# Two-layer graph network on one core: ScalarE copies the edge counts of sixteen destinations in one instruction instead of eight

## The reference, cut to what matters

```python
norm = dis[src] * dis[dst]
def _gcn(x, W, b, src, dst, norm):
    h = x @ W
    msg = h[src] * norm[:, None]
    out = jax.ops.segment_sum(msg, dst, num_segments=N)
    return out + b
h = jax.nn.relu(_gcn(x, W1, b1, src, dst, norm))
h = jax.nn.relu(_gcn(h, W2, b2, src, dst, norm))
return (x + h) * 0.5
```

## Time and profile before

| what | value |
|---|---|
| three runs | 1050.73, 1050.91, 1060.28 us; median 1050.91 |
| the profiled execution | 1058.88 us |
| its span, first to last instruction | 1057.0 us |
| mean granted TensorE clock | 0.956 of full speed |
| busy, TensorE matmuls / weight loads | 953.4 / 635.5 us |
| busy, VectorE / ScalarE / GpSimd | 698.6 / 591.3 / 442.9 us |
| copies out of the windows (L1611) | 784 instructions, 348.1 us |

### The profile page before, as it was taken

The page is one execution under the profiler, slowest core; times in us unless marked ns, Lnnn a source line. Parts: engine busy times, 40 slices in busy tenths (PEclk is TensorE's granted clock), DMA queues, the critical chain, the costliest instruction groups (busy, mean ns, idle before and its releaser), DMA issues.

```text
span 1057.0 us, 24147 instructions
## 1 busy us (share of the span) xinstructions
PE 953.4 (90%) x9848; PEld 635.5 (60%) x9848; DVE 698.6 (66%) x1238; ACT 591.3 (56%) x1322; POOL 442.9 (42%) x260
## 2 busy tenths in 40 slices
PE   5666677579979999999999999999999999999996
PEld 4566676466756666766666665555555555555554
DVE  5688788599969999999999990233333333333333
ACT  4999354289869989898988982112222222212212
POOL 3688304239864868959682000301222222212220
PEclk9898889659989999999999999999999999999997
DMA  9999999106663556666554501346766776777700
GB/s 326 385 389 378 361 323 319 34 27 197 223 226 118 173 162 223 223 223 198 165 173 154 186 2 36 111 153 232 240 232 231 238 239 232 239 239 239 240 27 18
DMA packets 196421, 214.97 MB, mean 203 GB/s; under 512 B 5359, under 2 KB 172421, under 8 KB 196174
## 3 DMA queue, kind: packets, MB, share of 16 engines
q1 hardware_dynamic: 190621, 201.05, 56.1%
q0 software_dynamic: 4944, 10.51, 3.1%
q10 hardware_dynamic: 737, 1.77, 0.4%
HBM read 137.71 MB, written 72.39 MB: 199 GB/s over the span
## 4 chain that ended last, share of the span: by engine, by line
PE 68%; POOL 6%; DVE 3%; ACT 3%; issue 1%; DMA 0%; POOLq 0%
PE dense_p L1655 44%; PE win_p L1647 10%; POOL ql L1314 4%; PE win_p L1745 4%; PE win_p L1736 2%; PE win_p L1753 2%; DVE st L1486 2%; POOL ql L1319 1%; ACT uv L1525 1%; PE lin_p L1712 1%; PE win_p L1721 1%; PE lin_p L1672 1%; DVE adj_all L1486 1%; ACT adj_all L1611 1%; PE code_p L1635 1%
## 5 line engine op out<-in xcount | busy, mean ns | idle before, releaser
L1611 ACT CAST adj_all<-win_p 128x392 f16<-128x392 f32 x784 | 348.1, 497 | 42.7 <-PE win_p L1647 17.5
L1655 PE MATMUL dense_p<-adj_all,g_all 128*128 128x448 f16 x1372 | 364.1, 352 | 0.2 <-ACT adj_all L1611 0.2
L1647 PEld LDWEIGHTS win_p<-adj_all,st 128*128 128x128 f16 x3136 | 215.6, 101 | 135.2 <-DVE adj_all L1486 17.8
L1655 PE MATMUL dense_p<-adj_all,total 128*128 128x448 f16 x1372 | 275.1, 353 | 0.0
L1647 PE MATMUL win_p<-adj_all,st 128*128 128x98 f16 x3136 | 256.7, 213 | 15.2 <-DVE adj_all L1486 9.9
L1486 DVE TENSOR_TENSOR st<-iota_lo,code 128x2048 f16<-128x2048 f16 x196 | 239.3, 1221 | 10.4 <-PE win_p L1647 5.6
L1655 PEld LDWEIGHTS dense_p<-adj_all,total 128*128 128x128 f16 x1372 | 133.0, 98 | 135.3 <-issue 26.6
L1486 DVE TENSOR_TENSOR adj_all<-iota_mv,code 128x1568 f16<-128x1568 f16 x196 | 191.6, 977 | 0.0
L772 PE MATMUL agg_p<-ahot,arows 128*64 128x64 f32 x3240 | 120.1, 241 | 40.3 <-issue 16.1
L772 PEld LDWEIGHTS agg_p<-ahot,arows 128*64 128x64 f32 x3240 | 114.6, 155 | 46.4 <-issue 45.8
L1319 POOL COPY ql<-loops 112x8 f32<-112x8 f32 x12 | 112.3, 9359 | 35.1 <-DMA ql<-ql_d,start_i 35.1
(11 more groups left out here) (233 smaller groups left out, 719.2 us busy)
## 6 DMA issues: line engine op xcount, KB each, us to landing
adj_d<-adj_all SPq DMA_DIRECT2D x12, 5488.0 KB, 18.9
adj_all<-adj_d SPq DMA_DIRECT2D x12, 5488.0 KB, 18.6
arows<-in_edge_attr_dram SPq DMA_DIRECT2D x45, 960.0 KB, 10.8
arows<-in_edge_attr_dram SPq DMA_DIRECT2D x9, 640.0 KB
uv<-agg SPq DMA_DIRECT2D x28, 112.0 KB, 2.7
h<-in_x_dram SPq DMA_DIRECT2D x4, 768.0 KB
xt<-in_x_dram SPq DMA_DIRECT2D x13, 224.0 KB, 2.9
arows<-in_edge_attr_dram SPq DMA_DIRECT2D x9, 320.0 KB
```

Of the source, the lines that this page charges most:

```text
L1611: nc.scalar.copy(adj[:, b % 2, :, j * GN + k * WN:j * GN + (k + 1) * WN], win_p[:, n % 4, 0:WP * MV].rearrange("p (h d) -> p h d", d=WN)). ...
L1647: ins = nc.tensor.matmul(win_p[:, n % 4, 0:WP * MV] .rearrange("p (h c t) -> p h c t", c=WP, t=PN)[:, :, c, :], st[:, i % 2, k // UW, pair ...
L1655: ins = nc.tensor.matmul(dense_p[:, half, 0:BN], g[:, c, s, :], adj[:, half, c, :], start=(c == 0 and s == 0), stop=(c == HI - 1 and s == 1))
```

## The change

ScalarE's loop over the windows of a group takes two at a time. It waits until both are built, copies the two neighbouring banks in one instruction with a source pattern of 49 x 2 x 8 (source pair of columns, window, destination) into 16 adjacent float16 destinations, and raises `evicted` by two. Since `n` is even there, the pair is in banks 0 and 1, or 2 and 3. TensorE's waits are as they were; but as `evicted` now grows by two, the window that is first in its pair waits in effect for the two windows four and three back. The general path for nodes of high degree (behind `act.If(rounds > 1)`) isn't touched and isn't run here.

```diff
-                            for k in range(GW):
+                            for k in range(0, GW, 2):
                                 n = b * WINDOWS + j * GW + k
-                                act.wait_ge(built, n + 1)
-                                nc.scalar.copy(adj[:, b % 2, :, j * GN + k * WN:j * GN + (k + 1) * WN],
-                                               win_p[:, n % 4, 0:WP * MV].rearrange("p (h d) -> p h d", d=WN)
-                                               ).then_inc(evicted, 1)
+                                act.wait_ge(built, n + 2)
+                                nc.scalar.copy(
+                                    adj[:, b % 2, :, j * GN + k * WN:j * GN + (k + 2) * WN]
+                                    .rearrange("p h (w d) -> p h w d", d=WN),
+                                    win_p[:, n % 4:n % 4 + 2, 0:WP * MV].rearrange("p w (h d) -> p h w d", d=WN)
+                                ).then_inc(evicted, 2)
```

## The result

| what | before | after |
|---|---|---|
| median of the comparison, us | 1054.56 (1050.73 to 1060.28, 4 runs) | 1070.63 (1069.73 to 1071.99, 4 runs) |
| ratio after / before | | 1.0117, 95% interval 1.0084 to 1.015 |
| the profiled execution, its span | 1058.88, 1057.0 | 1069.73, 1067.8 |

The change makes the kernel slower, by 1.2% as the recorded ratio has it. That isn't the ratio of the two medians, which would be 1.0152 (16.1 us): the four executions of the kernel before fall into two kinds, near 1051 and near 1059, and their median lies between them, where no execution does. Against the usual kind (1059, see the first experiment) the changed kernel takes 11.4 us more. Between the two profiled executions are 10.8 us of span.

The account below looks back on a forecast made before the run. TensorE was taken to bind, VectorE just ahead and ScalarE with 3 us idle per block. Terms 0.5 + 10.0 + 0.3 = 10.8 us, added to 1050.9 and rounded, gave 1062 us; range 1053 to 1077.

Parts of the forecast that it names:

- The price of a pair: On ScalarE, a 784-element pair copy takes 0.81 us, the next instruction following after 0.71; a single holds it 0.38.
- `high`, 0.66 per block: At `high`, the copy ahead holds ScalarE 0.33 us longer and the one behind takes 0.33 longer, delaying TensorE.
- `take_codes`, 0.09: At a block's start, the pair copy behind `take_codes` releases window 4 at 427.46 instead of 427.37, 0.09 us late.
- The borders, 0.04 each: At four group borders per block, TensorE needs 1.34 us where 1.30 are available: 0.04 us each, 0.16 per block.
- The border with `take_block`: Behind group 1, `take_block` stands between pair copies; window 4 comes at 435.59 instead of 435.55, 0.04 us late.
- The sum per block: Borders 0.16, block start 0.09 and `high` 0.66 make 0.91 us; blocks 3 to 13 pay in full, 10.0 us.
- the 0.3 of the end: At the end of block 13, the dense run's start waits for the last pair copy: 0.3 us more.
- the 0.5 for the blocks ahead: Blocks 1 and 2 mostly shorten TensorE's later wait for codes; only 0.5 us reaches VectorE over `add_bias` of block 2.
- The base: The loss of 10.8 us was added to 1050.9 us, the median of the runs shown, giving 1062.
- Rival 1, the two banks: Reading 8 elements from each bank in turn costs extra: a pair takes 0.97 us or more, time 1080; chance 0.17.
- Rival 2, VectorE hides it: VectorE is the real bound, so TensorE's later releases only eat slack: 1051 to 1053 us; chance 0.10.
- Rival 3, GpSimd's wait goes: A gap in VectorE lets block 4's codes come in time, removing the 6.42 us wait: near 1056 us; chance 0.09.

Follow-up runs that it names:

- the first experiment: The kernel before, unchanged, executed once more: 1059.69 us in the median of 12, beside 1059.19 of the 17 executions it was compared with.
- the spread kernels: `high` split into single activations behind windows of group 5, its cast in group 6: kernel before so edited 1079.25 us, changed kernel so edited 1075.18.
- where room is made on purpose: The kernel before plus one VectorE wait in block 2, ahead of group 6, leaving GpSimd a gap: 1051.59 us, ratio 0.9936.

## Why the prediction was right, and where it was off

- **Direction and size.** Forecast 10.8 us for one execution, 1058.88 to 1069.7; the profiled execution took 1069.73. The agreement to 0.03 us is luck: the blocks from 4 on cost 0.06 to 0.10 more each than in my sum, and block 3 (0.69 instead of 0.91, where the clock varies) and the parts ahead of the blocks and behind made up for it. The kernel before, profiled again, took 1062.51. By the ratio the change costs 1.2%, past the mark of 1% that I gave 0.53. The range holds the measured median.
- **The price of a pair.** Forecast 0.81 us and 0.71 to the next instruction; measured 0.813 and 0.71. The line between 392 and 896 elements held.
- **`high`, 0.66 per block.** Measured 0.70 by the two timelines, and 0.71 by the periods with pairs only there. The missing 0.05 is the start of the copy, below.
- **`take_codes`, 0.09.** Measured 0.10 to 0.11, from window 0 to the next group's window 0: 4.20 instead of 4.09.
- **The borders, 0.04 each.** Three of them measured 0.01 to 0.02. The copy starts 0.05 later than I had it, but TensorE, still in its large matmuls, starts the waiting window 0.06 behind the copy's end (455.52 to 455.58) and not 0.14, which is what it takes from rest. The border with `take_block` was mis-sized most: 0.04 forecast, 0.13 measured (window 0 to window 4 of group 2 takes 1.99 instead of 1.86). From window 7 of group 1 to window 4 of group 2 my sum had 0.38 + 0.71 + 0.42 + 0.95 = 2.46; the changed kernel has 436.83 to 437.27, 437.97, 438.40 and 439.37, so 0.44 + 0.70 + 0.43 + 0.97 = 2.54.
- **The sum per block.** 0.91 forecast, 0.97 to 1.01 measured in blocks 4 to 11. The term of 11 blocks and the end was 10.3, and measured 11.2; the 0.3 of the end measured 0.34 (1.30 behind window 7 instead of 0.96); the 0.5 for the blocks ahead measured 0.4 by the span from the first `turn_codes` to the one of block 3 (200.97 to 301.23, against 201.41 to 301.30).
- **The base was the step that was off.** I put the sum onto the median of three runs, 1050.9, and read the one at 1060.28 as the odd one. It was the other way: 1059 is the usual execution of the kernel before and the short one comes in 9 of 65. The forecast of 1062 was for a kind of execution that the changed kernel didn't show in its four runs; the measured 1070.63 is 1059.2 + 11.4. What the prediction couldn't see in the quick kind is now in part known: the wait of 6.4 us, for which it had no term beyond its length, brings some 1.4 us or more at the half clock with it.
- **Rival 1, the two banks,** fell with the 0.813 us of a pair, and the run that reads bank by bank took the same. **Rival 2, VectorE hides it,** fell: both periods grew by the whole loss, and VectorE's waits for TensorE grew from 7.3 to 18.6 us. But it was nearer than I had it. In the spread kernels VectorE and GpSimd do bind. **Rival 3, GpSimd's wait goes,** did not happen in the change (5.69 us are left of 6.42), but its mechanism is real: where room is made on purpose, 8.0 us go, and 6.4 was the price I had put on it; 1.4 of the rest is the clock.

## What to carry to other kernels

An instruction that does two steps' work saved its engine 0.05 us here, and cost the consumer the whole second step twice over where a queue stood: once ahead of the long work behind it, and once when the buffers were released in front of a waiting engine. Before merging, ask whether that engine is the bound; here it had 3 us of 30 free and the merge turned 37 us of its work into waiting. And where engines run this close to each other, price a change by the periods between undisturbed marks in the trace and not by totals alone, since a stall that flips on and off, and the clock behind it, can be larger than the effect.

## What the runs showed of the hardware that I had not expected

A pair copy starts 0.43 us behind its window where a single one starts 0.38 behind. The trace has an instruction of its own for its wait: on line 1610, the wait for `built`, the kernel before has 12 such (the ones that wait for two things) and the changed kernel 392, one per copy; first before, then after:

```profile
L1610 ACTq EVENT_SEMAPHORE  x12: 17/17/17, 265.4 to 608.4; - x12
```

```profile
L1610 ACTq EVENT_SEMAPHORE  x392: 17/17/38, 206.0 to 648.9; - x196
```

One more instruction of 17 ns and 0.05 us to the start, in the kernel that reads bank by bank too. It comes with the pair copies alone: the kernel with pairs only around `high` has both forms, and on the line of the pairs' wait 24 of them, one per pair:

```profile
L1611 ACTq EVENT_SEMAPHORE  x24: 17/17/17, 293.0 to 645.7; - x24
```

That it comes with the pattern of one dimension more is my reading; the pair copies also raise `evicted` by two, and no run varied either by itself.

GpSimd's instructions can be held off very long by VectorE: a copy of 8 elements per partition took 15.2 to 28.9 us beside back-to-back one-hot instructions, where in the spread kernel it also took 0.2 to 0.9, and an indirect DMA's issue 28.6 to 41.3, where it also took 0.9. The five that I followed through the rows ended in VectorE's next gap or beside an instruction of its that reads PSUM.
